# Layernorm transposes emptied by VectorE instead of ScalarE, and the score copy put ahead of the row maximum, in an 8-core attention kernel

## What is computed

```python
xn = layernorm(x)                        # over the 1024 features
Q = xn @ W1 + b1; K = xn @ W2 + b2; V = xn @ W3 + b3
attn = softmax(Q @ K.T / 32)             # 4096 x 4096 per batch element
a = (attn @ V) @ W4 + b4
f = complex_linear(xn; G1_R, G2_R, G1_I, G2_I)   # 1024 -> 1024, weights unfolded from G1, G2
out = x + a + f
```

## Time and profile before

| What | us |
|---|---|
| Median of the 2 timed runs | 1770.07 |
| The two runs | 1763.02 and 1777.13 |
| The profiled execution's own time | 1780.8 |
| Its span, first to last instruction, of the slowest core (core 0) | 1779.3 |
| Span of the other cores in it | 1757.1 to 1774.7 |
| PE busy on core 0 | 1593.2 (90%) |
| DVE busy | 697.3 (39%) |
| ACT busy | 564.1 (32%) |
| POOL busy | 128.6 (7%) |

### The profile page before, as it was taken

One profiled execution on the slowest core, in us unless ns is written; L12 is line 12 of the kernel. 1 busy time (PEld: TensorE's weight loads), 2 busy tenths in 40 slices (PEclk: granted clock), 3 DMA queues, 4 the chain that ended last, 5 costly groups with the idle time before them and its releaser, 6 DMA issues.

```text
span 1779.3 us, 25234 instructions; the slowest of 8 cores (1757.1 to 1779.3 us)
## 1 busy us (share of the span) xinstructions
PE 1593.2 (90%) x8496; PEld 781.2 (44%) x8496; DVE 697.3 (39%) x1607; ACT 564.1 (32%) x1129; POOL 128.6 (7%) x107
## 2 busy tenths in 40 slices
PE   2767989888899999999999999999999999999998
PEld 1423555555444444444444444444444444444443
DVE  1312111221245525443553445254434444443454
ACT  2102444444333232323233333332233233332322
POOL 2000111111100000100000000000000000000000
PEclk9679787899999999999999999999999999999999
DMA  9243111111411111101111111111111110110001
GB/s 175 40 73 46 48 49 51 68 48 48 142 36 36 36 36 36 39 33 39 46 60 36 36 36 36 36 36 36 36 36 48 36 48 24 60 37 24 25 24 36
DMA packets 69531, 83.48 MB, mean 47 GB/s; under 512 B 39699, under 2 KB 49947, under 8 KB 69406
## 3 DMA queue, kind: packets, MB, share of 16 engines
q1 hardware_dynamic: 56030, 42.01, 8.3%
q10 hardware_dynamic: 9216, 33.56, 5.9%
q0 software_dynamic: 4160, 6.29, 2.4%
HBM read 69.27 MB, written 18.87 MB: 50 GB/s over the span
## 4 chain that ended last, share of the span: by engine, by line
PE 86%; ACT 4%; DMA 3%; issue 3%; DVE 2%; ACTq 1%; POOL 0%; DVEq 0%; SPq 0%; POOLq 0%
PE po L658 13%; PE po L662 13%; PE po L557 12%; PE sp_a L557 6%; PE sp_b L557 6%; PE sp_a L422 4%; PE sp_b L422 3%; PE pf L587 3%; PE pf L446 3%; PE po L446 3%; PE sp_a L524 3%; PE sp_b L524 3%; PE ptA L629 2%; ACT QXT L402 2%; DMA xg<-x 2%
## 5 line engine op out<-in xcount | busy, mean ns | idle before, releaser
L658 PE MATMUL po<-V,ETs 128*128 128x512 bf16 x1024 | 391.9, 383 | 0.0
L662 PE MATMUL po<-V,ETs 128*128 128x512 bf16 x1024 | 391.6, 382 | 0.0
L557 PE MATMUL po<-KT,QXT 128*128 128x512 bf16 x1024 | 231.5, 379 | 0.0
L617 DVE TENSOR_REDUCE r<-Et 128x1 f32<-128x512 bf16 x256 | 173.9, 679 | 135.9 <-ACT Et L613 135.7
L378 POOL TENSOR_SCALAR xnn<-xg,rstd,nmr 128x1024 bf16<-128x1024 f32 x64 | 76.5, 1200 | 1321.6 <-DVE nmr L374 1321.6
L613 ACT ACTIVATE Et<-Ssb,ngm 128x512 bf16<-128x512 f32 x256 | 167.3, 710 | 12.9 <-PE ptB L629 11.3
L557 PEld LDWEIGHTS po<-KT,QXT 128*128 128x128 bf16 x1024 | 100.2, 98 | 120.8
L662 PEld LDWEIGHTS po<-V,ETs 128*128 128x128 bf16 x1024 | 101.0, 99 | 96.2 <-issue 3.3
L658 PEld LDWEIGHTS po<-V,ETs 128*128 128x128 bf16 x1024 | 100.8, 98 | 96.2 <-issue 3.0
L562 DVE TENSOR_REDUCE mx<-po 128x1 f32<-128x512 f32 x128 | 88.6, 692 | 132.5 <-PE po L557 132.5
L349 DVE BATCH_NORM_STATS2 bn<-xg 128x6 f32<-128x512 f32 x64 | 44.1, 690 | 240.9 <-DMA xg<-x 240.9
(11 more groups left out here) (92 smaller groups left out, 1838.7 us busy)
## 6 DMA issues: line engine op xcount, KB each, us to landing
xg<-x ACTq DMA_DIRECT2D x64, 512.0 KB, 3.6
xr<-x SPq DMA_DIRECT2D x32, 512.0 KB, 3.5
out<-xr SPq DMA_DIRECT2D x32, 512.0 KB, 2.6
KT<-W POOLq DMA_DIRECT2D x2, 2048.0 KB, 44.2
Ssb<-W SPq DMA_DIRECT2D x8, 512.0 KB, 7.6
Wproj<-W POOLq DMA_DIRECT2D x1, 2048.0 KB, 20.8
scr<-V SPq DMA_DIRECT2D x2, 1024.0 KB, 6.3
V<-scr SPq DMA_DIRECT2D x64, 32.0 KB, 2.9
```

The source lines that it names most:

```text
L557: P.add("tensor", lambda e, tb=tb, c=c, si=si, spv=spv: e.matmul(spv, QT[:, c, si * 128:(si + 1) * 128], KT[:, c, tb * 512:(tb + 1) * 512] ...
L617: P.add("vector", lambda e, tb=tb: e.reduce_sum(r8[:, tb:tb + 1], Et[:, tb % 4, :], axis=AX.X), waits=[("exp", i, tb)] + ([("rr", i - 1)] ...
L658: P.add("tensor", lambda e, tb=tb, q=q, tj=tj: e.matmul(po[:, 0:512], ETs[:, tb % 4, q, :], V0[:, tj, 0:512], start=(tj == 0), stop=(tj == ...
L662: P.add("tensor", lambda e, tb=tb, q=q, tj=tj: e.matmul(po[:, 512:1024], ETs[:, tb % 4, q, :], V0[:, tj, 512:1024], start=(tj == 0), stop= ...
```

## The change

Two edits. The first moves the 256 instructions of 128 x 256 at L402, which empty the layernorm transposes, from ACT (an `activation` with Identity) to DVE (a `tensor_copy`): four for each of 64 tiles, of which 36 tiles are transposed in the projection phase and 28 in the loop over `tb`. The second turns the order round in which the two readers of a score block may start. Before, DVE took the maximum first, ACT's copy waited for it, and the copy set the slot free. Now ACT's copy waits only for the matmuls, DVE's maximum waits for the copy, and the maximum sets the slot free.

```diff
-            P.add("scalar", lambda e, u=u, c0=c0, bank=bank: e.activation(
-                xnT[:, u, c0:c0 + 2, :], bank[:, :, :], AF.Identity),
+            P.add("vector", lambda e, u=u, c0=c0, bank=bank: e.tensor_copy(
+                xnT[:, u, c0:c0 + 2, :], bank[:, :, :]),
                 waits=[("xtp", gt, p4)], mark=("xte", gt, p4))
...
-                P.add("vector", lambda e, tb=tb, spv=spv: e.reduce_max(
-                    mx8[:, tb:tb + 1], spv, axis=AX.X),
-                    waits=[("Smm", i, tb)], mark=("Smx", i, tb))
-                scw_ = [("Smm", i, tb), ("Smx", i, tb)]
+                scw_ = [("Smm", i, tb)]
...
-                free[spk] = ("Scp", i, tb)
+                P.add("vector", lambda e, tb=tb, spv=spv: e.reduce_max(
+                    mx8[:, tb:tb + 1], spv, axis=AX.X),
+                    waits=[("Smm", i, tb), ("Scp", i, tb)],
+                    mark=("Smx", i, tb))
+                free[spk] = ("Smx", i, tb)
```

## The result

| | Kernel before | Changed kernel |
|---|---|---|
| Runs that are compared | 1762.9 to 1782.7 us | 1700.3 to 1703.0 us |
| Profiled execution, own time | 1780.8 | 1700.88 |
| Its spans by core | 1757.1 to 1779.3 | 1687.7 to 1699.3 |
| Ratio, 95% interval | | 0.9615 [0.9573, 0.9658] |

The changed kernel is faster by 3.9%, some 68 us. The plain median of its 11 runs, 1790.38, can't be read as its speed: in six of them one die had a clearly lower granted clock (0.80 to 0.93 as the mean of a core), as in one of the 10 runs of the kernel before, for a reason that no run here settles, and the ratio compares the others.

The account below looks back on a forecast made before the run. PE, busy for 90% of the span, was taken as the bound, so only its idle time and lost clock could be won: 28.6 + 14.4 + 4.5 + 10 = 57.5 us off 1770.1 gives 1712.6 us, range 1698 to 1736 (8 in 10).

Parts of the forecast that it names:

- Edit 1 in the attention phase: Attention phase, 28 layernorm tiles: two transpose rounds emptied by DVE take 1.66 us instead of 2.68; gain 28.6 us.
- Edit 1 in the projection phase: Projection phase, layernorm transposes behind V: the block takes 2.88 us instead of 3.99, 13 times; gain 14.4 us.
- The first group and the start: First projection group and program start: evictions no longer behind ACT's wait for a DMA, loads of x earlier; gain 4.5 us.
- The 3.0 from the loads: First group: ACT's queue issues loads of x 3.0 us earlier, no longer behind eight evictions of 0.38; gain 3.0 us.
- the 1.0 at the start: Program start: ACT issues loads up to 3.0 us earlier beside the weights' DMAs; gain between 0 and 3, taken as 1.0.
- The clock: Both phases: PE spends less time at 1.2 GHz behind waits; gain 10 us of 15 extra, bounds 0 to 15.
- the projection phase's share: Projection phase: six long intervals among 13, with PE at the lower clock, make some 8 us of extra time.
- The 0.86 for eight K matmuls: Projection phase: full-clock time of eight K matmuls, called half of sixteen in 3.45 us, against 1.91 at the lower clock.
- Edit 2 (0): Score blocks: swapped order makes the last block's first exponential 0.74 us later, hidden with about 1.3 to spare; cost 0.
- Rival B: Layernorm copies on DVE wait behind a sum of 0.69 us in all 41 blocks; 28 us come back, 1741; chance 0.08.
- Rival C: Last score block: the swap doesn't stay hidden, exponential 0 heads a chain; 24 us come back, 1737; chance 0.05.
- Rival D: Attention phase: denser work brings a granted clock between PE's levels; 1854 us if half the phase runs so; chance 0.04.

Follow-up runs that it names:

- the last experiment: Against the changed kernel: four transposes instead of two in each of ptA and ptB, and the b2 loads first on their own semaphore; 0.9352 of the kernel before, 1653.0 us.

## Why the prediction was right, and where not

**Direction, size, place: right.** 1712.6 was forecast, some 1700.5 measured, within 1698 to 1736. The gain was 68 us instead of 57.5.

**Edit 1 in the attention phase (28.6).** Measured 26.8. The two rounds take 1.64 (forecast 1.66), and exponential 6 is out of the way; moving it alone, and putting its wait back alone, show that this is the cause. The step that is off is small: a tile gains 0.96, not 1.02, since the second pair of block 6's transposes starts later behind the first (947.04 and 947.23 in the changed kernel, 0.11 apart before).

**Edit 1 in the projection phase (14.4).** The block is 2.88, as forecast to the hundredth. The half group gains 1.23, not 1.11; the first K evictions used to stand behind the last L402 on ScalarE, and now don't. Before, the third eight K matmuls, which need the first eight's buffer back, began 0.99 behind the second eight, where the other distances are 0.87 or 0.88; in the changed kernel this one is 0.87 too. This 0.12 was missing.

**The first group and the start (4.5).** 5.6 in the first group, and nothing measurable at the start, where cores and executions differ by up to 10 us. Two terms there were mis-sized. The 3.0 from the loads is one. The load is still what binds the tile after (PE waits 1.5 to 1.8 us for POOL at its transposes), but ScalarE's queue issues it 9.0 us behind the first V instead of 13.8 to 14.0: it had stood behind eight evictions that in turn waited for PE's transposes, and that is 4.8 us, not their own 8 x 0.38. So PE starts these transposes some 5 us earlier, and V of tile 2 starts 9.9 us behind V of tile 0 instead of 13.5. And the 1.0 at the start isn't there, because K's first eviction hangs on a small load which the change doesn't touch.

**The clock (10, bounds 0 to 15): the term that was mis-sized.** Measured 16.9, just outside the bounds. The step that failed was the projection phase's share ("and make some 8 us"): it took the projection phase's extra time from core 0, which from 180 to 340 us had a granted clock of 0.78 anyway. The other cores lost 11.4 us there. And I expected a third of the loss to stay, and nearly none does. The runs show the tie to the waits from both sides: with PE's block at 1.79 or 1.64 us the attention phase loses under 1 us; with 2.68 it loses 5 to 9, and 7 to 10.5 with the swap alone; with the wait put back (2.75) 2 to 24. (The 0.86 for eight K matmuls is a quarter of the 3.45, not a half; the reading of the lower clock stands.)

**Edit 2 (0).** Right: 1.0002 alone. The 0.74 that the first exponential would be late was 0.71.

**Rival B** (VectorE late at the copies, 28 us back) is refuted by its idle time of 1.46 ahead of the first copy. **Rival C** (the swap not hidden) is refuted by the run with the swap alone. **Rival D** (a granted clock between the levels in the attention phase) did not come in the profiled execution: 1.00 on all eight cores. The rule of the Trainium skill beside it ("TensorE: Matmul & The Clock Gate", Seeing it yourself), a limit of 13/16 for a whole die under dense matmuls on three or more of its cores, is not borne out by the profiled executions, with all eight cores busy: not at 97% busy in the attention phase here, nor with the still denser kernel of the last experiment.

## What to carry to other kernels

When an engine executes strictly in order, look at what stands *behind* an instruction that waits for another engine. Four short evictions cost PE about 0.9 us a time (2.68 against 1.79) because an exponential that was long ready stood behind them; moving the exponential ahead gave most of that phase's gain without touching any engine's load. Then count the clock: what PE lost behind such stretches of waiting was a quarter of the whole gain here (16.9 of 65), and it shows in PE's busy time, not in its waits. And where a pair of buffers in turn is what is left, make each buffer's load larger: one copy of 512 columns took 0.42 us, two of 256 took 0.57.

## What the runs showed of the hardware that I had not expected

- PE's clock is lost without any single long wait. Before, in the projection phase, about every second half group ran on at 1.2 GHz for a while behind a block of 3.99 us whose waits were 1.32, 0.45 and 0.45 us; the loss was 1.54 us each time, 11 to 12 us on each core that ran at the full clock otherwise. Behind the block of 2.88 us it happened at most once in 13.
- The loss is unsteady: a stretch of 2.75 us with a longest wait of 1.46 gave 2 to 24 us on the eight cores of one execution, where 2.68 with 1.23 gave 5 to 9; a stretch of 1.79 gave none.
- Small loads at the start take long to land: the last of 23 small ones on SyncE's queue was issued at 21 to 27 us, and what waited for it began at 43 to 52 (both in the profiles of the two kernels of this study). With eight of them put first, K's evictions started at 35 to 38.
